# Three prefetches at the segment boundaries of a selective scan, and the order of the tensor work in its last stage

## The reference

```
xi, z = split(x @ in_proj_w)                 # 2 x 2048 channels
xi = silu(causal_conv4(xi) + conv_b)
dt, Bm, Cm = split(xi @ x_proj_w)            # 64, 16, 16
dt = softplus(dt @ dt_proj_w + dt_proj_b)
h_t = exp(dt*A) * h_(t-1) + (dt*u) * Bm_t    # 16 states per channel
y = (sum_n h*Cm + u*D) * silu(z)
fg = sigmoid(x @ fg_w + fg_b)
x1 = layernorm(x + fg*x + (1-fg)*(y @ out_proj_w))
best_p = max(softmax(x1 @ Wg + bg))
out = layernorm(x1 + (x1 @ We + be) * best_p)
```

## Time and profile before

| | before |
|---|---|
| median of three runs | 6730.53 us |
| the profiled execution's own time | 6735.53 us |
| its span on the slowest core | 6734.0 us (8 cores: 6695.0 to 6734.0) |
| VectorE busy | 4804.5 us (71%) |
| TensorE busy | 2186.1 us (32%) |
| ScalarE busy | 1720.1 us (26%) |
| DMA, mean over the span | 33 GB/s |

### The profile page before, as it was taken

The page is one execution under the profiler, slowest core; times in us unless marked ns, Lnnn a source line. Parts: engine busy times, 40 slices in busy tenths (PEclk is TensorE's granted clock), DMA queues, the critical chain, the costliest instruction groups (busy, mean ns, idle before and its releaser), DMA issues.

```text
span 6734.0 us, 26158 instructions; the slowest of 8 cores (6695.0 to 6734.0 us)
## 1 busy us (share of the span) xinstructions
PE 2186.1 (32%) x7184; PEld 748.5 (11%) x7184; DVE 4804.5 (71%) x2836; ACT 1720.1 (26%) x1830; POOL 0.2 (0%) x4
## 2 busy tenths in 40 slices
PE   0677721222221122222112212211222221687785
PEld 0233300000000000000000000000000000222231
DVE  1555518888883788888478888856888886356565
ACT  0333313232321223232123232321323231122121
POOL 0000000000000000000000000000000000000000
PEclk9999965555565555555555555555555555788887
DMA  4222260000003100000410000021000002211110
GB/s 109 75 63 75 63 83 9 10 14 9 14 9 46 22 9 14 9 14 9 42 27 10 9 14 9 14 34 30 14 10 14 10 14 96 80 40 60 53 50 25
DMA packets 144973, 221.66 MB, mean 33 GB/s; under 512 B 23904, under 2 KB 73056, under 8 KB 142688
## 3 DMA queue, kind: packets, MB, share of 16 engines
q1 hardware_dynamic: 144832, 220.01, 13.6%
HBM read 152.57 MB, written 67.40 MB: 33 GB/s over the span
## 4 chain that ended last, share of the span: by engine, by line
DVE 65%; PE 14%; issue 6%; DMA 6%; SPq 4%; ACT 2%; another core or an unknown queue 1%; DVEq 1%; ACTq 0%
DVE hbg L76 33%; DVE dubg L76 9%; DVE prodg L76 9%; PE psN L76 4%; SPq L76 4%; DVE cacc L76 4%; PE psY L76 3%; DMA zsb<-z_hbm 3%; PE psA L76 3%; DVE xln L76 2%; PE psS L76 2%; DVE ln L76 2%; DVE y L76 1%; ACT tmpb L76 1%
## 5 line engine op out<-in xcount | busy, mean ns | idle before, releaser
L76 DVE TENSOR_TENSOR_SCAN hbg<-dabg,dubg 128x4100 bf16<-128x4100 f32 x256 | 2227.2, 8700 | 27.4 <-DVE dubg L76 1.4
L76 PE MATMUL psY<-prodg,ident 128*128 128x512 bf16 x2048 | 900.1, 619 | 3807.4 <-DVE dubg L76 3143.7
L76 ACT ACTIVATE dabg<-dt,acol 128x1024 f32<-128x1024 f32 x1024 | 1084.4, 1136 | 1351.0 <-DVE hbg L76 735.1
L76 PEld LDWEIGHTS psY<-prodg,ident 128*128 128x128 bf16 x2048 | 263.6, 138 | 4437.7 <-issue 4437.7
L76 DVE TENSOR_TENSOR prodg<-hbg,warena 128x4096 bf16<-128x4096 bf16 x256 | 587.2, 2294 | 37.4 <-DVE hstate L76 12.3
L76 PE MATMUL psA<-xb,warena 128*128 128x512 bf16 x2048 | 484.0, 393 | 377.9 <-DVE xb L76 203.2
L76 DVE TENSOR_TENSOR dubg<-dub,warena 128x4096 bf16<-128x4096 bf16 x256 | 587.1, 2293 | 26.6
L76 ACT ACTIVATE rawb<-psD,dtbc 128x1024 f32<-128x1024 f32 x64 | 71.3, 1115 | 1891.3 <-PE psD L76 1889.8
L76 DVE TENSOR_TENSOR dub<-dt,usb 128x1024 bf16<-128x1024 f32 x64 | 78.4, 1225 | 445.1 <-DMA zsb<-z_hbm 438.9
L76 DVE SCALAR_TENSOR_TENSOR cacc<-xi_pad,cw,cacc 128x512 bf16<-128x512 bf16 x384 | 288.5, 751 | 41.5 <-DVE cacc L76 1.8
L76 PE MATMUL psN<-ybufc,warena 128*128 128x512 bf16 x1024 | 259.9, 412 | 138.9 <-DVE xbC L76 136.8
(11 more groups left out here) (75 smaller groups left out, 1656.5 us busy)
## 6 DMA issues: line engine op xcount, KB each, us to landing
warena<-xdblb_hbm SPq DMA_DIRECT2D x16, 2048.0 KB, 69.6
wstage<-w_in SPq DMA_DIRECT2D x16, 1024.0 KB, 6.0
xs<-x_fm SPq DMA_DIRECT2D x8, 2048.0 KB, 13.2
u_hbm<-ub SPq DMA_DIRECT2D x32, 512.0 KB, 5.1
z_hbm<-z_all SPq DMA_DIRECT2D x32, 512.0 KB, 6.1
usb<-u_hbm SPq DMA_DIRECT2D x64, 256.0 KB, 2.9
zsb<-z_hbm SPq DMA_DIRECT2D x64, 256.0 KB, 3.2
y_hbm<-ybf SPq DMA_DIRECT2D x64, 256.0 KB, 2.0
```

Source lines behind the costliest of these rows:

```text
L76: ins = real(*a, **kw)
```

## The change

Two edits, and nothing else.

**Stage B.** `segsB` and its loop are gone. A segment is now written out whole: its four warena DMAs, its own glue of block 0, then the blocks, where the last block has no glue ahead of it. So at each of the three boundaries between segments the next segment's glue of block 0, with its pair of u and z loads, stands behind the last block's gloop and the warena DMAs, and no longer ahead of that gloop. The first segment's order is what it was.

**Stage C.** In `merge` the alternation of `post` (F3 to F7) with tail A is replaced by F3, the first seven chunks of tail A, F4 to F7, and the feed-forward.

```diff
-            segsB = [seg_funcs(b, sh)
-                     for b in range(BLOC) for sh in range(S // SH)]
-            segsB[0][0]()
-            segsB[0][1](0)
-            for si, (dmas_f, glue_f, gloop_f) in enumerate(segsB):
-                for dc in range(NDC):
-                    if dc + 1 < NDC:
-                        glue_f(dc + 1)
-                    elif si + 1 < len(segsB):
-                        segsB[si + 1][1](0)
-                    gloop_f(dc)
-                if si + 1 < len(segsB):
-                    segsB[si + 1][0]()
+                    emit_glue(0)
+                    for dc in range(NDC):
+                        if dc + 1 < NDC:
+                            emit_glue(dc + 1)
+                        emit_gloop(dc)
...
-                i = j = 0
-                while i < len(post) or j < len(ta):
-                    if i < len(post):
-                        out.append(post[i]); i += 1
-                    if j < len(ta):
-                        out.append(ta[j]); j += 1
+                if post:
+                    out.append(post[0])
+                out.extend(ta[:7])
+                out.extend(post[1:])
+                out.extend(ta[7:])
```

More of the change, by code:

```diff
@@ L498, in build_nc @@
                     serial=False)
-            def seg_funcs(b, sh):
+            for b in range(BLOC):
+                for sh in range(S // SH):
                     h0 = sh * SH
                     col0 = b * S + h0
[L504 to L514, removed]
+                    wab = warena[:, :]
+                    for grp in range(4):
+                        r0 = grp * 8
+                        xh = xdblb_hbm[r0, col0:col0 + SH]
+                        df.dma([(RawAP(wab.tensor, wab.offset + r0 * SH,
+                                       [[32832, 128], [SH, 8], [1, SH]]),
+                                 RawAP(xh.tensor, xh.offset,
+                                       [[0, 128], [BLOC * S, 8], [1, SH]]))],
+                               reads=[("xdblh",)],
+                               writes=[("wa", r0 + j) for j in range(8)])
                     def emit_glue(dc):
@@ L645, in emit_gloop @@
                                reads=[("ybf", dpar)], writes=[("yh", b, dc, sh)])
-                    return emit_dmas, emit_glue, emit_gloop
-            segsB = [seg_funcs(b, sh)
-                     for b in range(BLOC) for sh in range(S // SH)]
-            segsB[0][0]()
-            segsB[0][1](0)
-            for si, (dmas_f, glue_f, gloop_f) in enumerate(segsB):
-                for dc in range(NDC):
-                    if dc + 1 < NDC:
-                        glue_f(dc + 1)
-                    elif si + 1 < len(segsB):
-                        segsB[si + 1][1](0)
-                    gloop_f(dc)
-                if si + 1 < len(segsB):
-                    segsB[si + 1][0]()
+                    emit_glue(0)
[3 more added lines that the diff above has]
+                        emit_gloop(dc)
             df.flush(block)
```

## The result

| | before | changed |
|---|---|---|
| median | 6733.19 us (6725.46 to 6746.4, 8 runs) | 6901.5 us (6891.64 to 6937.79, 8 runs) |
| ratio | | 1.0257, 95% interval [1.0238, 1.0276] |
| the profiled execution's own time | 6735.5 us | 6905.8 us |

What follows compares the result with a forecast made beforehand. It took VectorE's scans to bound stage B, and TensorE and VectorE waiting in turns stage C. Stage C +170.5 us and boundaries -3.0 gave +167.5: 6903 us for the profiled execution, 6900 forecast, range 6862 to 6935.

Steps and rivals of the forecast that it cites:

- What bounds the kernel: Stage B bound by VectorE's scans with holes at segment starts; in stage C TensorE and VectorE take turns, neither full.
- The tail from the cast: Stage C, from the xlnb cast's end to the next xbC cast: 62.0 us against 39.2, +22.8 an iteration.
- F4: Stage C's first matmul group behind the softmax's broadcast starts at the low clock: 7.0 us, against 5.2 without that.
- feed-forward: Stage C, VectorE behind gate 1: 16.5 us with the third product at the low clock, 14.3 without a fall.
- The broadcasts: Stage C, mrow to reciprocal: two small float32 broadcasts at the lower clock, 9.40 us against 7.11, +2.3 an iteration.
- iteration 1: Stage C iteration without tail B: reciprocal 2.7 us sooner, then +22.8, so +20.1 us.
- The boundaries: Stage B's three segment boundaries: -6.6 us ahead, +5.6 behind the landing, -1.0 each; -3 us in all.
- the upper bound: Boundaries: a second queued load pair delays each landing by 1.8 us, as at stage B's start; +2.4 us in all.
- The clock costs nothing new: Rival for stage C: no added low-clock cost, 6.3 us less in seven iterations, 6856 us; chance 0.06.
- The clock stays low: Rival for stage C: F4 to F7 all run at the low clock, +21.9 us times seven, 7053 us; chance 0.04.
- Faster: Rival for stage C: F4 to F7 run while VectorE does norm and softmax, about -16 us, 6720; chance 0.03 with its like.

Runs made afterwards that it cites:

- e2: The kernel before with only the change's stage C order (the `merge` part), boundaries as before: 6884.44 us, ratio 1.0253.
- e5: The kernel before with F6, F7 and gate 1 moved behind the softmax, F4 and F5 left beside the norm: 6820.19 us, ratio 1.0159.
- e1: The kernel before with only the change's stage B edit at the segment boundaries: 6714.80 us, ratio 1.0001.
- e8: The kernel before with the change's stage B order, but the next block 0's u and z loads still ahead of the last gloop: 6704.19 us, ratio 0.9987.
- e3: The kernel before with gate 1 alone moved behind the softmax, F4 to F7 still interleaved with tail A: 6714.48 us, ratio 1.0010.
- e9: The changed kernel with unused filler matmuls in three TensorE pauses, more of them than e4 has: 6843.15 us, ratio 1.0177.
- e6: The kernel before with gate 1's four operations dealt one by one into VectorE's waits in the softmax: 6672.82 us, ratio 0.9931.
- e4: The changed kernel with unused filler matmuls (40, 14 and 36) in three TensorE pauses of iterations 1 to 7: 6854.85 us, ratio 1.0200.
- e7: e6 with each segment's four warena DMAs split around the last block, two issued inside its gloop: 6374.98 us, ratio 0.9455.

## Why the prediction was right

It said 6900 us; the median is 6901.5, and for the profiled execution it said 6903 where 6905.8 was measured.

**What bounds the kernel.** Right. e2 shows that stage C's order alone carries the loss, and e5 that each group of matmuls taken from beside VectorE's work costs its own length.

**The tail from the cast.** Predicted 62.0 us, measured 62.2 in iteration 2. Its terms: logits 1.5 (1.49 measured), softmax 8.6 (8.77) and broadcast 2.0 (1.97), F4 7.0 (7.42), F5 to F7 15.5 (15.54), evictions 1.5 (1.54), gate 9.4 (9.40), feed-forward 16.5 (16.03). F4 was sized by iteration 0 and came out 0.4 too small. Such a start scatters: the first 16 matmuls of iteration 0 took 5.44 us before, 6.51 in the changed kernel and 6.05 in e5. The feed-forward was 0.5 too large, by two errors that partly cancel. The third product starts 1.8 us behind the gate (6065.67) and not 0.9, because it waits for the addition that follows the first ffnb and not only for the ffnb; the fourth ffnb comes 1.7 us behind the third (6069.13 to 6070.86) and not 2.8.

**The broadcasts.** The mis-sized term. The measured 9.04 us is near the 9.40 of the earlier trace rows, but I measured the gain from iteration 2, whose 7.11 is the second lowest of six: before they were 7.11, 7.10, 8.48, 7.50, 8.08 and 7.20, mean 7.58. So it is +1.5 an iteration and not +2.3. With it the sum is 24.3, and the casts say 24.0 (140.04 against 116.09). Over six iterations the forecast was 6.7 us too high; iteration 0, +2.1 and not forecast, and iteration 1, +20.9 against +20.1, give some back: stage C +167.2 against +170.5.

**The boundaries.** The mechanism was right in both halves: the memset stands right behind ybf, and 5.6 us have come in behind the landing, which e1 and e8 show. With the landings taken off, the stretch between two boundaries is 1079.6 us before and 1078.6 with the change (means over eight cores), the -1.0 of the sum. The forecast was -3 us and the measured +2.0 ahead of stage C's start, inside the bounds of -3 to +2.4: the three landings took 111.7, 114.4 and 112.5 us against 111.9, 111.9 and 110.9. That is the scatter of a landing, as e1 to e3 show, and not the second pair; the upper bound's reason, the 1.8 us of stage B's start, was not one (e1). The two errors, -3.3 in stage C and +5 in stages A and B, nearly cancel; part of the closeness is luck.

**The rivals.** The clock costs nothing new (6856): refuted by F4, the third product and the broadcast, all measured slow, and by e9, where all three are fast when TensorE has just worked (5.19 us, 3.61 us for 16 matmuls, 1.09 us). Its price of 6.3 us an iteration was too high: the terms measured add up to 5.2 (broadcasts 1.5, F4 2.2, feed-forward 1.5), because the broadcasts had been slow in part before too and the feed-forward loses 1.5 and not 2.2. The clock stays low (7053): refuted, F5 to F7 take 15.54 us. Faster (6720): the matmuls stand behind the broadcast, and TensorE runs in order. The condition was right to be asked for, though: what e6 fills, the softmax's waits, is where the faster kernel was.

**Left open.** What sets the length of a slow start: the first 16 matmuls of iteration 0 took 5.25 us in e4 and 6.51 in the changed kernel, behind pauses of 87.3 and 88.2 us. And why a landing scatters, and is longer at stage B's start than at the boundaries.

## What to carry to other kernels

Where two engines wait for each other in turns, read for each block of work what it stood beside, and charge a moved block its full length if its new place has nothing beside it: here 4 groups of matmuls, 22.5 us, were charged once for each iteration, and the busy totals had shown nothing of it. Size a term by the mean over the iterations, not by the one that was followed. For a gain look for the opposite: pieces of the busy engine's own work dealt out into its waits (-0.7% in e6), and large loads split so that each part starts when its own buffer rows are done with (-5.5% with e7, most of it at the boundaries).

## What the runs showed of the hardware

I had thought of TensorE's pauses of 9 to 40 us alone. But the 1x512 float32 broadcast took 2.04 us behind a pause of 3.12 us (e4), with the granted clock at 0.96 over the pause and 0.50 behind it, and 1.09 us behind one of 0.31 us (e9). The last pause alone doesn't decide it: behind 1.05 to 1.12 us of idle time the second broadcast took 1.09 us in the kernel before's iteration 2 and 2.02 us in e5's. A group of 24 matmuls, 5.18 us at the high level (granted clock 1.00, 2.4 GHz), took 6.58 us as F4 in e4 and 7.42 in the changed kernel, and the group behind it 5.2 in both.

The landing behind four 2 MB loads took 98 to 114 us at the boundaries and 108 to 117 at stage B's start, over all eight cores of every kernel here but e7; a few us between two of them are no evidence. With two such loads at a time and not four (e7), one took 43.0 us from issue to landing by the page's median, and 69.6 in the kernel before.
